# Attention on TensorE: both score products first, then both raw tiles

## The chip, the cores and the metric

The kernel runs on one NeuronCore of a Trainium2 chip. The metric is the device time of one execution in microseconds; lower is better. Times of single instructions come from one profiled execution, which takes a little longer than the median of the unprofiled runs.

## What is computed

Two transformer layers on x of shape (8, 512, 256), each with an attention and a feed-forward part that a modulation vector scales and shifts. The part that matters here is the attention, once in each layer, 16 heads of 16 features, over 8 batches of 512 tokens:

```
q, k, v = h @ wq.T, h @ wk.T, h @ wv.T          # first layer: then rms, rope on q and k
scores = einsum('bhtd,bhsd->bhts', q, k) * scale
attn = softmax(scores, axis=-1)
y = einsum('bhts,bhsd->bhtd', attn, v)
```

The softmax needs the maximum of each query's row of scores.

## The kernel before

`program` runs `attention` for the first layer, `mlp0`, `attention` for the second layer and `experts` in turn. Each `attention` call writes one long instruction list for every engine by a loop over steps p; every engine has its own `step(p)`, and semaphores tie them together.

A step works on a pair of heads. A pair's two heads lie in the two halves of the rows of KT and QS: head a = 0 in rows 0 to 48, head a = 1 in rows 64 to 112 (`BLK * a`). 32 steps make a batch (PAIRS), 8 steps a group of four heads, called G. For a group the scores are computed twice:

- **raw(n)**, line 1068: for query tile tt and head a of a pair, the unscaled scores with queries on the output's rows, 128x512, into SM[:, n % 2]. VectorE takes the negated row maximum of it (**maximum**, line 853). Once 16 maxima of a group are there, VectorE turns them (line 860) and eight DMAs of SyncE's queue write them as one more row of QS (line 348). Step p issues raw 2p + 28 and 2p + 29 (AHEAD is 28), so the maxima run 14 steps ahead of their use. Raw n waits until the maximum of n - 2 is done (line 1064): SM has two buffers.
- **scores(S, a)**, line 1084: the transposed scores of step S, with the extra row of maxima as a 49th row of the product, into ST[:, u % 2, a]. ScalarE turns both heads' scores into P in one exponential of 128x1024 (line 624). The call with a = 1 comes first and holds the waits: for the exponential two steps back (line 1081), and in the first step of a group for the DMAs of the maxima (line 1079).

Behind these four products a step of TensorE issues what its place in the batch asks for, here called its block: `job` (projections to q, k, v, transposes; placed by the tables AT0 and AT1), **values** (line 1101, four column tiles of P by V, in the steps 3, 5, 6 and 8 of a group), or the transposes of y (line 1143, in step 9, so step 1 of the next group). VectorE's step takes, in this order, the normalising work on AV (lines 888 and 894, in step 10, so step 2), the layer norm's statistics, the maximum of raw 2p + 28, in one step of a group the turning of the maxima, and the maximum of raw 2p + 29; in the first layer copies and reductions stand around them (lines 879, 919, 924).

Raws go from n = 0 to 511, so steps -14 to 241 have raws; scores go from step 0 to 255. Both are in steps 0 to 241.

```
if n >= 2:
    pe.wait_ge(max_s, n - 1)
r = slice(BLK * a, BLK * a + 3 * HD)
nc.tensor.matmul(SM[:, n % 2, :], QS[b % 2][r, 2 * g + pair, tt * 128:tt * 128 + 128],
                 KT[b % 2][r, 2 * g + pair, :], start=True, stop=True).then_inc(raw_mm, 1)
```

In a step n is even for the first raw, which has a = 0, and odd for the second, which has a = 1.

Of the kernel before, what the change touches and what calls it, by code (L numbers as in the profile page):

```python
# [109 lines left out]
AHEAD = 28  # L110
# [48 lines left out]
def attention(nc, layer, d, keep, ahead=None):  # L159
# [4 lines left out]
    def slots_of(name, n):  # L164

        return EARLY[n][name] if n < len(EARLY) and name in EARLY[n] else tuple(PAIRS * n + o for o in AT[name])
# [18 lines left out]
    def group_at(p, late):  # L185

        G, r = divmod(p - late, 8)
        return G if r == 0 and 0 <= G < B * NG else None

    with ExitStack() as ctx:  # L190
# [60 lines left out]
        def out(name, n):  # L251

            done_sem, out_sem, k = turn_of(name, n)
            return out_sem, k
# [711 lines left out]
        def tensor_steps(pe):  # L966
# [87 lines left out]
            def raw(n):  # L1054

                if not 0 <= n < 16 * B * NG:
                    return
                G, t = divmod(n, 16)
                b, g = divmod(G, NG)
                pair, a, tt = t // 8, t % 2, (t % 8) // 2  # L1060
                if g == 0 and t == 0:
                    pe.wait_ge(qk_ld[b % 2], 192 * (b // 2 + 1))
                if n >= 2:
                    pe.wait_ge(max_s, n - 1)
                elif n == 0 and L0:
                    pe.wait_ge(*out("H3", 0))
# [4 lines that stand above are left out]
            def scores(S, a):  # L1071

                G, u = divmod(S, 8)
                b, g = divmod(G, NG)
                if L0 and S == 0 and a == 1:
                    pe.wait_ge(*out("V1", 0))
                    pe.wait_ge(*out("QK3", 1))
                if u == 0 and a == 1:
                    pe.wait_ge(row_ld[G % 2], 128 * (G // 2 + 1))
                if S >= 2 and a == 1:  # L1080
                    pe.wait_ge(exp_s, S - 1)
                pair, o = 2 * g + u % 2, (u // 2) * 128
                r = slice(BLK * a, BLK * a + QROWS)
                ins = nc.tensor.matmul(ST[:, u % 2, a, :], KT[b % 2][r, pair, o:o + 128], QS[b % 2][r, pair, :],  # L1084
                                       start=True, stop=True)
                if a == 0:
                    ins.then_inc(st_mm, 1)

            def values(G, st):

                b, g = divmod(G, NG)
                pe.wait_ge(exp_s, 8 * G + 2 * st + 2)
                if st == 0:
                    if g == 0:
                        pe.wait_ge(*out("V1", b))
                    if G >= 1:
                        pe.wait_ge(y_out, G)
                    elif L0:
                        pe.wait_ge(mod_moved, 3)
                for j in range(HG):  # L1100
                    ins = nc.tensor.matmul(AV[32 * j:32 * j + 32, :], V[b % 3][:, st, g * HG + j, :], P[:, st, j, :],  # L1101
                                           start=st == 0, stop=st == TT - 1)
                ins.then_inc(av_mm, 1)

            def modulation(i):

                l, m0, m1, to = mod_part[i]
                pe.wait_ge(wm_ld[i], 16)
                if i == 2:
                    pe.wait_ge(*out("H1", 0))  # L1110
                for m in range(m0, m1):
                    for k in range(FT):
                        ins = nc.tensor.matmul(to[:, (m - m0) * B:(m - m0) * B + B], wm[:, l, k, m * 128:m * 128 + 128], cs[:, l, k, :],
                                               start=k == 0, stop=k == FT - 1)
                ins.then_inc(mod_mm, 1)
# [6 lines left out]
            def step(p):  # L1122
                if L0 and p in MOD_AT:
                    modulation(MOD_AT.index(p))
                raw(2 * p + AHEAD)
                if 0 <= p < PAIRS * B:
                    scores(p, 1)
                    scores(p, 0)
                raw(2 * p + AHEAD + 1)
                name, n = jobs.get(p, ("", 0))  # L1130
                if name:
                    job(name, n, (0, 1) if len(slots_of(name, n)) == 1 else (1,))
                elif p in begun:
                    job(*begun[p], (0,))
                for st, late in enumerate((3, 5, 6, 8)):
                    G = group_at(p, late)
                    if G is not None:
                        values(G, st)
                G = group_at(p, 9)
                if G is not None:  # L1140
                    pe.wait_ge(y_cp, G + 1)
                    for tt in range(TT):
                        ins = nc.tensor.transpose(AV[:, tt * 128:tt * 128 + 128], ysb[:, tt * 128:tt * 128 + 128], id32[:, :])
                    ins.then_inc(y_mm, 1)
                if group_at(p, 10) is not None and PAIRS * B - 58 <= p < PAIRS * B - 12 and p not in jobs and p not in begun:
                    free = jobs[max(q for q in jobs if q < p)]
                    pe.wait_ge(*out(*free))
                    src = wp_h[:, :, :].rearrange("p k n -> p (k n)") if L0 else keep["spare2"][:, 0:T]
                    for k in range(3):
                        nc.tensor.matmul(X[:, :], id16[:, :], src, start=True, stop=True)  # L1150
# [1289 lines left out]
```

## Time and profile before

| | |
|---|---|
| median of 3 runs | 1984.94 us (1984.57 to 1988.12) |
| the profiled execution | 1994.66 us |
| its span, first to last instruction | 1993.0 us |
| TensorE busy | 1820.3 us (91%) |
| VectorE busy | 1345.1 us (67%) |
| ScalarE busy | 1150.1 us (58%) |
| GpSimd busy | 654.5 us (33%) |
| mean granted TensorE clock | 0.954 |
| row maxima, line 853 | 1024, 654.4 us, 683 ns each |
| exponentials, line 624 | 512, 523.6 us, 1025 ns each |
| raws, line 1068 | 1024, 354.9 us busy |
| scores, line 1084 | 1024, 300.3 us busy |
| values, line 1101 | 2048 records, 275.2 us busy |

Shares are over the whole span, which has stages with different limits: the first attention call has scores from 108.0 us on, the second until 1681.9. Busy times of one line are times in which at least one of its instructions ran; TensorE overlaps its products, so the sum over lines says little of its pace. A product with values is recorded twice. Idle time is put down to what ended it.

### The profile page before, as it was taken

The page shows a single profiled execution, that of the slowest core. Times are in us where ns is not written, and L with a number is a line of the kernel's source. Part 1 is how long each engine was busy: PE and PEld are TensorE (multiplying, and loading weights), DVE is VectorE, ACT ScalarE, POOL GpSimd, SP SyncE. Part 2 cuts the span into 40 slices and gives each one's busy share as a digit, 9 for nine tenths or more (in the row PEclk, how much of TensorE's full clock was granted, in tenths as well). Part 3 has the DMA queues.
Part 4 walks back from the last instruction along what each step waited for, and adds up shares of the span by engine and source line. Part 5 has one row for each costly group of instructions (what it writes and reads, how often), then busy time and mean ns, then how long its engine had stood idle before and what let it go on. Part 6 is the DMA issues. An engine that isn't in the chain of part 4 may idle for free. (4 is left out here: it accounts for less than half of the span.)

```text
span 1993.0 us, 29496 instructions
## 1 busy us (share of the span) xinstructions
PE 1820.3 (91%) x10344; PEld 754.6 (38%) x10344; DVE 1345.1 (67%) x2598; ACT 1150.1 (58%) x1553; POOL 654.5 (33%) x918
## 2 busy tenths in 40 slices
PE   4789999999979999999999997899999997499998
PEld 3323333332224444444444443223233322355554
DVE  5488889888744535535535542688888884689993
ACT  4368778876743333424334232478778776477774
POOL 5667687761220000000000112234444311335452
PEclk8689999999989999999999998699999999699999
DMA  3345545444262000000001004333332320624410
GB/s 118 64 93 123 136 120 123 107 108 99 86 219 98 22 11 12 22 1 22 22 1 48 11 11 75 53 75 71 68 67 59 65 38 29 232 79 144 158 44 32
DMA packets 119620, 147.65 MB, mean 74 GB/s; under 512 B 19779, under 2 KB 102838, under 8 KB 117430
## 3 DMA queue, kind: packets, MB, share of 16 engines
q1 hardware_dynamic: 119478, 145.79, 27.7%
q8 instruction: 85, 1.39, 0.3%
q14 instruction: 57, 0.47, 0.1%
HBM read 100.34 MB, written 45.14 MB: 73 GB/s over the span
## 5 line engine op out<-in xcount | busy, mean ns | idle before, releaser
L853 DVE TENSOR_REDUCE A_M<-A_SM 128x1 f16<-128x512 f32 x1024 | 654.4, 683 | 137.8 <-PE A_SM L1068 135.2
L624 ACT ACTIVATE A_P<-A_ST 128x1024 f32<-128x1024 f32 x512 | 523.6, 1025 | 166.1 <-PE A_ST L1084 161.8
L1068 PE MATMUL A_SM<-A_KT,A_QS 48*128 48x512 f16 x1024 | 354.9, 399 | 45.2 <-DVE A_M L853 37.5
L1619 PE MATMUL B_PA<-B_Hh,B_wh 128*128 128x512 f16 x1024 | 388.1, 379 | 3.1 <-DVE B_Hl L1584 3.1
L1619 PE MATMUL B_PA<-B_Hl,B_wh 128*128 128x512 f16 x1024 | 388.1, 379 | 0.0
L1538 ACT ACTIVATE B_af<-B_PA,B_sv 128x512 f32<-128x512 f32 x192 | 131.9, 687 | 357.2 <-PE B_PA L1619 357.0
L1084 PE MATMUL A_ST<-A_QS,A_KT 49*128 49x512 f16 x1024 | 300.3, 386 | 2.6 <-DMA A_QS<-A_rows 2.1
L1101 PE MATMUL A_AV<-A_P,A_V 128*32 128x512 f32 x2048 | 275.2, 609 | 4.2 <-ACT A_P L624 3.6
L1582 DVE TENSOR_SCALAR B_Hh<-B_af 128x512 f16<-128x512 f32 x128 | 62.8, 490 | 278.8 <-ACT B_af L1538 278.8
L1068 PEld LDWEIGHTS A_SM<-A_KT,A_QS 48*128 48x128 f16 x1024 | 83.3, 93 | 432.7 <-DVE A_M L853 382.1
L1333 POOL TENSOR_TENSOR B_hl<-B_hf,B_hh 128x512 f16<-128x512 f32 x14 | 16.2, 1156 | 506.4 <-ACT B_hh L1349 506.4
L1619 PEld LDWEIGHTS B_PA<-B_Hh,B_wh 128*128 128x128 f16 x1024 | 100.2, 98 | 122.2 <-DVE B_Hl L1584 3.6
L1619 PEld LDWEIGHTS B_PA<-B_Hl,B_wh 128*128 128x128 f16 x1024 | 100.2, 98 | 118.8
L1584 DVE SCALAR_TENSOR_TENSOR B_Hl<-B_af,B_Hh 128x512 f16<-128x512 f32 x128 | 88.6, 692 | 4.4
L1101 PEld LDWEIGHTS A_AV<-A_P,A_V 128*32 128x32 f32 x2048 | 40.5, 108 | 79.5 <-issue 63.6
L972 PE MATMUL A_X<-A_wh,A_hh 128*128 128x256 f16 (+1 forms) x160 | 51.5, 322 | 12.6 <-ACT A_V L663 7.4
L1084 PEld LDWEIGHTS A_ST<-A_QS,A_KT 49*128 49x128 f16 x1024 | 55.4, 94 | 18.1 <-ACT A_P L624 9.4
L1538 ACT ACT_TABLE_LOAD x23 | 29.5, 1283 | 56.2 <-PE B_PA L1619 42.9
L1576 DVE SCALAR_TENSOR_TENSOR B_uf<-B_PD,B_sv,B_af 128x512 f32<-128x512 f32 x64 | 47.8, 746 | 18.9 <-ACT B_af L1538 13.7
L2249 PE MATMUL D_PA<-D_gh,D_eh 128*128 128x512 f16 x128 | 49.5, 386 | 4.9 <-POOL D_gl L1929 4.9
L516 POOL TENSOR_TENSOR A_ysq<-A_yn 128x256 f32<-128x256 f32 x32 | 19.6, 612 | 101.5 <-DVE A_yn L894 101.5
L2141 DVE SCALAR_TENSOR_TENSOR D_Hl<-D_af,D_Hh 128x512 f16<-128x512 f32 x64 | 43.0, 713 | 14.6 <-ACT D_Hh L2002 14.5
(362 smaller groups left out, 3246.1 us busy)
## 6 DMA issues: line engine op xcount, KB each, us to landing
D_w_st<-in_we_dram SPq DMA_DIRECT2D x16, 1024.0 KB, 7.2
qk<-A_tr SPq DMA_DIRECT2D x58, 256.0 KB, 2.5
A_KT<-qk SPq DMA_DIRECT2D x96, 128.0 KB, 5.0
A_QS<-qk SPq DMA_DIRECT2D x96, 128.0 KB, 4.9
A_w_st<-in_w_ffn_dram SPq DMA_DIRECT2D x32, 352.0 KB, 3.4
A_QS<-A_rows SPq DMA_DIRECT2D x512, 0.5 KB
w_hi<-A_f_hi SPq DMA_DIRECT2D x32, 176.0 KB, 3.4
w_lo<-A_f_lo SPq DMA_DIRECT2D x32, 176.0 KB, 3.9
```

Source lines behind the costliest of these rows:

```text
L624: nc.scalar.activation(P[:, st, 2 * pair:2 * pair + 2, :], ST[:, u % 2, :, :], ACT.Exp, scale=1.0 / math.sqrt(HD)).then_inc(exp_s, 1)
L853: nc.vector.tensor_reduce(M[G % 2][:, o:o + 1], SM[:, n % 2, :], AX, ALU.max, negate=True).then_inc(max_s, 1)
L972: ins = nc.tensor.matmul(out, a, c, start=first and n_ == 0, stop=last and n_ == len(todo) - 1)
L1068: nc.tensor.matmul(SM[:, n % 2, :], QS[b % 2][r, 2 * g + pair, tt * 128:tt * 128 + 128], KT[b % 2][r, 2 * g + pair, :], start=True, stop=T ...
L1084: ins = nc.tensor.matmul(ST[:, u % 2, a, :], KT[b % 2][r, pair, o:o + 128], QS[b % 2][r, pair, :], start=True, stop=True)
L1101: ins = nc.tensor.matmul(AV[32 * j:32 * j + 32, :], V[b % 3][:, st, g * HG + j, :], P[:, st, j, :], start=st == 0, stop=st == TT - 1)
L1538: nc.scalar.activation(af[:, s % 3, :], PA[:, s % 4, :], ACT.Silu if s < HM else ACT.Gelu, scale=sv[:, which, m:m + 1]).then_inc(a_out, 1)
L1576: nc.vector.scalar_tensor_tensor(out=uf[:, s % 2, :], in0=PD[:, s % 2, :], scalar=sv[:, 1, s:s + 1], in1=src, op0=ALU.mult, op1=ALU.mult). ...
L1582: nc.vector.tensor_scalar(Hh[w][:, m, :], src, HS, None, ALU.mult).then_inc(high, 1)
L1584: nc.vector.scalar_tensor_tensor(out=Hl[w][:, m, :], in0=src, scalar=HS, in1=Hh[w][:, m, :], op0=ALU.mult, op1=ALU.subtract).then_inc(spli ...
L1619: ins = nc.tensor.matmul(out, a, c, start=start and kt == 0 and n_ == 0, stop=stop and kt == kts[-1] and n_ == len(ops) - 1)
L2249: ins = nc.tensor.matmul(out, a, c, start=start and n_ == 0, stop=stop and n_ == len(ops) - 1)
```

## The change

In TensorE's `step`, the first raw moves behind the two scores. Nothing else is changed.

```diff
             def step(p):
                 if L0 and p in MOD_AT:
                     modulation(MOD_AT.index(p))
-                raw(2 * p + AHEAD)
                 if 0 <= p < PAIRS * B:
                     scores(p, 1)
                     scores(p, 0)
+                raw(2 * p + AHEAD)
                 raw(2 * p + AHEAD + 1)
                 name, n = jobs.get(p, ("", 0))
                 if name:
```

The order of the other engines and queues is the same. On TensorE, in the second call, at the first step of a group and the one behind it (A_SM is the raw tile, A_ST the scores, A_AV the values, A_X the bank of the jobs; A0_max counts VectorE's maxima, A0_row_ld the DMAs of the row of maxima, A0_exp the exponentials), before:

```order
L1068 MATMUL A_SM<-A_KT,A_QS 128x512 [waits A0_max]
L1084 MATMUL A_ST<-A_QS,A_KT 128x512 [waits A0_exp,A0_row_ld1]
L1084 MATMUL A_ST<-A_QS,A_KT 128x512
L1068 MATMUL A_SM<-A_KT,A_QS 128x512 [waits A0_max]
L1101 MATMUL A_AV<-A_P,A_V 32x512 [waits A0_exp]
L1101 MATMUL A_AV<-A_P,A_V 32x512 x3
L1068 MATMUL A_SM<-A_KT,A_QS 128x512 [waits A0_max]
L1084 MATMUL A_ST<-A_QS,A_KT 128x512 [waits A0_exp]
L1084 MATMUL A_ST<-A_QS,A_KT 128x512
L1068 MATMUL A_SM<-A_KT,A_QS 128x512 [waits A0_max]
```

and with the change:

```order
L1084 MATMUL A_ST<-A_QS,A_KT 128x512 [waits A0_exp,A0_row_ld1]
L1084 MATMUL A_ST<-A_QS,A_KT 128x512
L1068 MATMUL A_SM<-A_KT,A_QS 128x512 [waits A0_max] x2
L1101 MATMUL A_AV<-A_P,A_V 32x512 [waits A0_exp]
L1101 MATMUL A_AV<-A_P,A_V 32x512 x3
L1084 MATMUL A_ST<-A_QS,A_KT 128x512 [waits A0_exp]
L1084 MATMUL A_ST<-A_QS,A_KT 128x512
L1068 MATMUL A_SM<-A_KT,A_QS 128x512 [waits A0_max] x2
L1045 MATMUL A_X<-id,A_yn 128x128 [waits A0_y_out,A0_job_out]
```

The raw that stood ahead of the scores, and of their wait for the exponential and the row of maxima, now stands behind both; the two raws with their waits for the maxima are neighbours (x2), and the values follow the second raw as before.

Two steps on, where a projection with three products follows, before:

```order
L1068 MATMUL A_SM<-A_KT,A_QS 128x512 [waits A0_max]
L1084 MATMUL A_ST<-A_QS,A_KT 128x512 [waits A0_exp]
L1084 MATMUL A_ST<-A_QS,A_KT 128x512
L1068 MATMUL A_SM<-A_KT,A_QS 128x512 [waits A0_max]
L972 MATMUL A_X<-A_hh,A_wh 128x512 [waits A0_h_low,A0_job_out]
L972 MATMUL A_X<-A_hl,A_wh 128x512
L972 MATMUL A_X<-A_hh,A_wl 128x512
```

and with the change:

```order
L1084 MATMUL A_ST<-A_QS,A_KT 128x512 [waits A0_exp]
L1084 MATMUL A_ST<-A_QS,A_KT 128x512
L1068 MATMUL A_SM<-A_KT,A_QS 128x512 [waits A0_max] x2
L972 MATMUL A_X<-A_hh,A_wh 128x512 [waits A0_h_low,A0_job_out]
L972 MATMUL A_X<-A_hl,A_wh 128x512
L972 MATMUL A_X<-A_hh,A_wl 128x512
```

The first raw has changed places with the two scores; the block of projections keeps its place behind the second raw.

## Rows read from the trace of the kernel before

**Rows 1.** Stages: us from the start: length, busy us (instructions), clock, DMA share, GB/s
```profile
108.00:540.00 432.00, 404.70 (x2709) 128.97 (x2708) 376.46 (x696) 333.72 (x439) 264.96 (x317) 0.98 0.47 113
1269.50:1665.00 395.50, 375.22 (x2496) 114.83 (x2496) 333.36 (x622) 303.05 (x359) 131.02 (x266) 0.99 0.31 61
```

**Rows 2.** Who waited for whom, 1269.5 to 1665: us, times, longest
```profile
ACT A_P L624 <- PE A_ST L1084: 78.4, 131, 1.8
DVE A_M L853 <- PE A_SM L1068: 58.9, 124, 2.1
```

**Rows 3.** Who waited for whom, 108 to 540
```profile
DVE A_M L853 <- PE A_SM L1068: 39.5, 84, 2.2
```

**Rows 4.** Timeline, TensorE, second call: start us, us, instruction, [idle before]
```profile
1364.38 0.39 PE L1068 MATMUL A_SM<-A_KT,A_QS 48*128 48x512 f16 x1
1364.38 0.60 PE L1084 MATMUL A_ST<-A_QS,A_KT 49*128 49x512 f16 x2
1364.61 0.38 PE L1068 MATMUL A_SM<-A_KT,A_QS 48*128 48x512 f16 x1
...
1365.92 0.39 PE L1068 MATMUL A_SM<-A_KT,A_QS 48*128 48x512 f16 x1
1366.15 0.39 PE L1068 MATMUL A_SM<-A_KT,A_QS 48*128 48x512 f16 x1
...
1367.70 0.39 PE L1068 MATMUL A_SM<-A_KT,A_QS 48*128 48x512 f16 x1
1367.93 0.38 PE L1068 MATMUL A_SM<-A_KT,A_QS 48*128 48x512 f16 x1
...
1369.27 0.39 PE L1068 MATMUL A_SM<-A_KT,A_QS 48*128 48x512 f16 x1
1369.87 0.39 PE L1068 MATMUL A_SM<-A_KT,A_QS 48*128 48x512 f16 x1
...
1371.41 0.38 PE L1068 MATMUL A_SM<-A_KT,A_QS 48*128 48x512 f16 x1
...
1372.48 0.39 PE L1068 MATMUL A_SM<-A_KT,A_QS 48*128 48x512 f16 x1
1372.96 0.39 PE L1068 MATMUL A_SM<-A_KT,A_QS 48*128 48x512 f16 x1
1374.27 0.39 PE L1068 MATMUL A_SM<-A_KT,A_QS 48*128 48x512 f16 x1
...
1376.04 0.39 PE L1068 MATMUL A_SM<-A_KT,A_QS 48*128 48x512 f16 x1
1377.76 0.39 PE L1068 MATMUL A_SM<-A_KT,A_QS 48*128 48x512 f16 x1
```

**Rows 5.** Timeline, VectorE, the same group
```profile
1364.81 1.29 DVE L853 TENSOR_REDUCE A_M<-A_SM 128x1 f16<-128x512 f32 x2 [0.67 <-PE A_SM L1068]
...
1368.44 0.68 DVE L853 TENSOR_REDUCE A_M<-A_SM 128x1 f16<-128x512 f32 x1
```

**Rows 6.** Timeline of the first call, VectorE, and one row of TensorE
```profile
334.41 0.65 DVE L853 TENSOR_REDUCE A_M<-A_SM 128x1 f16<-128x512 f32 x1
...
336.60 0.68 DVE L919 TENSOR_REDUCE A_rv<-A_sq 128x32 f32<-128x512 f32 x1
...
338.88 0.69 DVE L853 TENSOR_REDUCE A_M<-A_SM 128x1 f16<-128x512 f32 x1 [0.41 <-PE A_SM L1068]
...
335.12 0.39 PE L1068 MATMUL A_SM<-A_KT,A_QS 48*128 48x512 f16 x1
```

**Rows 7.** The line of the scores, whole span: idle until, us, times
```profile
  DMA A_QS<-A_rows: 5.6, 9
```

**Rows 8.** Groups by line, 1269.5 to 1665: busy us, mean ns, idle before
```profile
L1101 PE MATMUL A_AV<-A_P,A_V 128*32 128x512 f32 x960 | 128.7, 608 | 0.0
```

**Rows 9.** Timeline, TensorE's weight loads, second call
```profile
1377.76 0.09 PEld L1068 LDWEIGHTS A_SM<-A_KT,A_QS 48*128 48x128 f16 x1 [0.42 <-DVE A_M L853]
1377.76 0.11 PEld L1084 LDWEIGHTS A_ST<-A_QS,A_KT 49*128 49x128 f16 x2
```

## The prediction

> **What bounds the kernel now.** I read the stage view first, then who waits for whom in each attention stretch, then the timeline of one group of eight steps. The change touches only the steps that issue both scores and raws: steps 0 to 241 of each of the two attention calls, 242 steps or 30.25 groups of eight per call. By the stage view [rows 1] these take 432.0 us in the first call and 395.5 us in the second, with TensorE busy 94% and 95% of that and VectorE 87% and 84%, at a granted clock of 0.98 and 0.99. A busy TensorE there is an engine that has something in it, not one at its peak, so the waits decide. In the second call VectorE's row maxima sat idle until TensorE's raw product 124 times, 58.9 us in all [rows 2]; in the first call 84 times, 39.5 us [rows 3]. So neither engine runs without a break: they hand two buffers (the two halves of SM) back and forth. I call the raw of the even number A and the other B.
>
> **The loop, in numbers.** All from one group of the second call, steps 0 to 7 from 1364.38 [rows 4]. (1) A and the first score start together (1364.38), the second score and B together 0.23 later (1364.61): they lie in different halves of the rows, so four products cost two slots of 0.23 us. (2) The maximum of A starts 0.43 after A (1364.81) [rows 5]. (3) Two maxima in a row take 1.29 us, one 0.69, so the second starts 0.60 after the first [rows 5]. (4) A raw that waits for its buffer starts 0.06 after the maximum that frees it: 334.41 + 0.65 = 335.06, the raw at 335.12 [rows 6]. A maximum's start to the raw that follows in its buffer is 0.68 + 0.06 = 0.74. (5) From B to the next step's first product is the step's own block: 1.31 with values, 1.55 with the transposes of step 1, 1.34 and 1.07 with three products in steps 2 and 4, 1.72 with six in step 7 [rows 4].
>
> If no product waits, B of the next step can't start before A + 0.43 + 0.60 + 0.74 = A + 1.77. That is the one limit that the change moves.
>
> **The change, part by part.** It adds and removes nothing; instruction counts, operands, DMAs and the orders of VectorE, ScalarE and the queues stay. Four products still make two pairs from different halves: both scores, then both raws. Cost of the pairs themselves: 0. What moves is A: it now starts 0.23 behind the step's first product, B where it was. Before, A and B were 0.23 apart and the scores filled that; VectorE got A first and was at work on it while B ran. Now both raws come together, and VectorE, which takes 0.60 per tile, gets its first tile 0.23 later.
>
> Worked for a step whose start P nothing delays. Before: A = P, so the next B is free at P + 1.77, and wants to start at P + 0.23 + block + 0.23; it waits if the block is under 1.31. After: A = P + 0.23, so B is free at P + 2.00 and wants the same place; it waits if the block is under 1.54. A block of values (1.31), half of all steps, just fits before and costs 0.23 after. In the step behind such a wait A and B are 0.23 apart again, the maxima start no later against B than before, and the next B waits for nothing new. So of a run of such steps about every second one pays 0.23.
>
> The whole group by this recurrence, starting with both buffers free (VectorE idle, as it is at 1364.38; step 2's first maximum is held by the normalising work ahead of it, to 0.74 after the step's start at 1367.70 [rows 4, 5]):
>
> | step | start before | waits of B | start after | waits of B |
> |---|---|---|---|---|
> | 0 | 0.00 | 0 | 0.00 | 0 |
> | 1 | 1.54 | 0 | 1.54 | 0.23 |
> | 2 | 3.32 | 0 | 3.55 | 0 |
> | 3 | 4.89 | 0.40 | 5.12 | 0.40 |
> | 4 | 6.83 | 0 | 7.06 | 0 |
> | 5 | 8.13 | 0.24 | 8.36 | 0.47 |
> | 6 | 9.91 | 0 | 10.37 | 0 |
> | 7 | 11.45 | 0 | 11.91 | 0.23 |
> | end | 13.40 | | 14.09 | |
>
> The trace has 1377.76 - 1364.38 = 13.38 for it, and the waits of B at steps 3 and 5 (0.60 and 0.48 from A to B in place of 0.23 [rows 4]), so the recurrence holds for before. It gives **+0.69 us per group**: three payments of 0.23. The same working with empty blocks in steps 2, 4 and 7, as at the end of the call, gives +0.69 too, since the payments sit in the same places.
>
> Second call: 30.25 x 0.69 = 20.9 us. First call: here VectorE has more to do between the maxima. Around 336.60 a further reduction of 0.68 us keeps it from idling until 338.88, where it waits 0.41 for a raw [rows 6]. While it is behind, it takes A late anyway and the 0.23 is hidden by its own backlog; the same recurrence over the group from 328.60 pays once, +0.23. I scale by the stalls: 84 against 124, 0.69 x 84 / 124 = 0.47 a group, 14.1 us. Bounds for the first call are 0.23 and 0.69 a group, 7 and 21 us.
>
> Side effects. The scores of a group's first step wait for the row of maxima that a DMA brings; that wait now holds A as well, which used to go ahead of it. It occurs 9 times, 5.6 us in all [rows 7]; what A could do meanwhile is at most 0.23 each, so 0 to 2 us, taken as 0 because the DMA chain itself starts with the same maxima. The exponential starts up to 0.23 earlier in its step. Nothing gains: the products with values, which need it, waited 0.0 us in all in the second call [rows 8].
>
> Sum: 20.9 + 14.1 = **+35 us**. On the profiled execution's own 1994.66 us (span 1993.0) that is 2029.7; this execution lies 9.7 above the median of the runs, 1984.94, so the median should be **2020 us**, 1.8% more.
>
> **A rule against the trace.** The second score's weights are in the same rows as those of A, which runs when they are loaded (1377.76, both score loads within 0.11 us), and the pairs still follow at 0.23 [rows 9, 4]. So a weight load behind a product in the same rows costs nothing here. The Trainium skill (TensorE: Matmul & The Clock Gate, section The mechanism) says that a weight load overlaps a running product only when the row group differs. By that rule the new order, in which the second score and A share a half and stand next to each other, would expose one load per step. The trace speaks against it for the old order, which has the same neighbours one product further apart.
>
> **Rivals.**
> - *The load shows.* If A's load can't start under the second score, each of the 484 steps takes the 0.09 us of one load more [rows 9]: 484 x 0.09 = 44 us on top, 2064. Chance 0.04.
> - *Hidden anyway.* Where VectorE never idles the delay costs nothing, as in five of the eight steps from 328.60. If my 0.06 and 0.43 are a little too long, the values block covers the delay: about 1985. Against it: 208 stalls that start exactly when a raw is done. Chance 0.06.
> - *Faster: ScalarE is what paces.* It sat idle before the exponential for 78.4 us, 131 times, in the second call until scores were done [rows 2]. If the chain scores, exponential, values ended last, each such wait would shrink by the 0.23 by which the second score moves ahead: 131 x 0.23 = 30 us, twice that for both calls, 1925. It decides from the point at which the values wait for the exponential; they waited 0.0 us [rows 8]. Chance 0.05.
> - *Every stall pays.* All (124 + 84) stalls grow by 0.23 and none is absorbed: 48 us, 2033; with the 2 us of the rows, 2035. Chance 0.05, the range's upper end.
>
> **How the numbers follow.** The forecast and the band around it have 0.80. Its low end is two payments a group in the second call (0.46 x 30.25 = 14 us) and none in the first: 1999, rounded down to 1998 for the runs' own scatter. The range 1998 to 2035 holds 0.85, the forecast and the last rival, and leaves out the three others. A measurement here can tell 0.2% (4 us) from no change: slower 0.89 (forecast, the load, every stall), same 0.06, faster 0.05.
>
> **What would show it.** Right: in the second call a group like the one from 1364.38 takes about 14.1 us in place of 13.4; VectorE's idle time behind raws grows by some 20 us there and about 14 in the first call, with more waits of TensorE before B; both raws start together after a long block, the first maximum 0.66 behind the step's start; the stretches without raws are unchanged. Wrong: an idle time of VectorE that stays near 59 and 40 us, pairs further apart than 0.23, values that wait for the exponential, or a longer time in the other stages.

## The result and the profile after

The change made the kernel slower: 2010.75 us (median of 4 runs, 2008.82 to 2012.26) against 1984.76 us (4 runs, 1983.48 to 1988.12), a ratio of 1.0116 with a 95% interval of 1.0095 to 1.0138. That is +26 us, where +35 was forecast. The profiled execution took 2011.95 us, with a span of 2010.2, 1.2 above its median; that of before lay 9.9 above its own. So the two traces differ by 17.3 us only, and they have to be compared stage by stage, and where the granted clock was the same.

The stages of the changed kernel (length, busy us of TensorE, weight loads, VectorE, ScalarE, GpSimd, then clock, DMA share, GB/s). First and third are steps 0 to 241 of the two attention calls; the second reaches from the end of the first call to the first raw of the second, the last from the last scores to the end:

```profile
109.70:546.80 437.10, 410.64 (x2709) 132.71 (x2708) 376.39 (x695) 331.86 (x439) 265.26 (x317) 0.99 0.46 112
565.20:1241.10 675.90, 650.03 (x3101) 306.30 (x3097) 310.71 (x636) 235.55 (x332) 45.85 (x53) 0.99 0.12 37
1268.90:1684.40 415.50, 391.63 (x2499) 119.24 (x2496) 333.95 (x623) 302.23 (x360) 131.01 (x266) 0.99 0.29 58
1701.20:2010.20 309.00, 264.75 (x1474) 148.96 (x1470) 233.60 (x442) 195.06 (x299) 133.66 (x169) 0.94 0.32 114
```

Of before the two attention stretches are [rows 1], and the two others:

```profile
558.60:1237.80 679.20, 650.28 (x3101) 306.34 (x3097) 314.47 (x636) 235.55 (x332) 45.60 (x53) 0.99 0.12 36
1681.90:1993.00 311.10, 267.85 (x1474) 150.24 (x1470) 233.56 (x442) 195.08 (x299) 134.01 (x169) 0.91 0.33 113
```

The second call's stretch grew from 395.5 to 415.5 us, the first call's from 432.0 to 437.1. TensorE's busy time grew along (375.2 to 391.6 in the second call), though its products are the same: it has something in it for longer. The untouched stages are 3.3 and 2.1 us shorter in this execution, the last at a granted clock of 0.94 in place of 0.91; that isn't the change's doing, and it is a part of what the traces lack against the medians.

The clock hides a part of the first call's loss as well. One group of eight steps of it (its 24th), before and with the change, in the columns of the rows above; the third number from the end is the granted clock:

```profile
442.72:458.75 16.03, 13.59 (x77) 3.05 (x77) 13.09 (x25) 8.70 (x10) 6.70 (x6) 0.79 0.67 215
447.48:461.02 13.54, 11.12 (x78) 3.10 (x78) 12.55 (x24) 7.93 (x10) 6.84 (x6) 1.00 0.66 206
```

The first ran 6.8 us of its time at the lower of the clock's two levels (1.2 GHz), the second none; a raw had waited 1.43 us for a maximum just before, at 448.54. This isn't tied to the order either: e1 below, as fast as the kernel before, took 13.03 us for this group at full clock.

The call's first group ran 10.9 us at the lower level before and 8.9 with the change (18.47 and 17.12 us in all). From step 0 to step 240, the first call ran 17.7 us at the lower level before and 8.9 with the change. So its growth over these 30 groups, 429.6 to 433.8 us, is too small a number for what the order costs.

The 28 groups that ran wholly at full clock in both traces are 8.0 us longer in sum, 0.28 a group. Against the kernel before, the same 28 groups are 8.0 us longer in e2 and 8.3 in e10, which have the new order in the first call, and 0.5 and 0.6 us shorter in e1 and e5, which lack it there (e5 has the old order in this call, e1 has A between the scores). In the second call 28 groups at full clock are 16.6 us longer, 0.59 a group. Taken for 30 groups each, that makes 8.5 and 17.7, an estimate of 26 us: what the medians differ by.

Who waited for whom in the second call's stretch, against [rows 2]:

```profile
DVE A_M L853 <- PE A_SM L1068: 80.5, 130, 2.8
ACT A_P L624 <- PE A_ST L1084: 80.3, 111, 1.8
```

and in the first call's, against [rows 3]:

```profile
DVE A_M L853 <- PE A_SM L1068: 51.3, 102, 1.2
```

VectorE's idle time behind raws rose by 21.6 us in the second call (58.9 to 80.5) and by 11.8 in the first (39.5 to 51.3). Now the group that the prediction worked through, TensorE from 1369.54 (of before: [rows 4]):

```profile
1369.54 0.39 PE L1084 MATMUL A_ST<-A_QS,A_KT 49*128 49x512 f16 x2
1369.77 0.38 PE L1068 MATMUL A_SM<-A_KT,A_QS 48*128 48x512 f16 x2
1370.08 1.06 PE L1101 MATMUL A_AV<-A_P,A_V 128*32 128x512 f32 x8
1371.08 0.39 PE L1084 MATMUL A_ST<-A_QS,A_KT 49*128 49x512 f16 x2
1371.31 0.61 PE L1068 MATMUL A_SM<-A_KT,A_QS 48*128 48x512 f16 x2
1371.85 0.66 PE L1045 MATMUL A_X<-id,A_yn 128*128 128x128 f32 x4
1372.34 0.60 PE L1143 MATMUL A_AV<-id,A_ysb 128*128 128x128 f32 x4
1372.88 0.39 PE L1084 MATMUL A_ST<-A_QS,A_KT 49*128 49x512 f16 x2
...
1374.43 0.39 PE L1084 MATMUL A_ST<-A_QS,A_KT 49*128 49x512 f16 x2
...
1376.36 0.39 PE L1084 MATMUL A_ST<-A_QS,A_KT 49*128 49x512 f16 x2
...
1377.65 0.39 PE L1084 MATMUL A_ST<-A_QS,A_KT 49*128 49x512 f16 x2
1377.88 0.86 PE L1068 MATMUL A_SM<-A_KT,A_QS 48*128 48x512 f16 x2
1379.67 0.39 PE L1084 MATMUL A_ST<-A_QS,A_KT 49*128 49x512 f16 x2
1379.89 0.38 PE L1068 MATMUL A_SM<-A_KT,A_QS 48*128 48x512 f16 x2
...
1381.20 0.39 PE L1084 MATMUL A_ST<-A_QS,A_KT 49*128 49x512 f16 x2
1381.43 0.61 PE L1068 MATMUL A_SM<-A_KT,A_QS 48*128 48x512 f16 x2
...
1383.38 0.39 PE L1084 MATMUL A_ST<-A_QS,A_KT 49*128 49x512 f16 x2
```

Both raws are one row (x2) at 1369.77, 0.23 behind the scores, and VectorE's first maximum starts at 1370.19, 0.65 after the step's start, where it was 0.43 [rows 5]:

```profile
1370.19 1.29 DVE L853 TENSOR_REDUCE A_M<-A_SM 128x1 f16<-128x512 f32 x2 [0.89 <-PE A_SM L1068]
1371.72 1.29 DVE L853 TENSOR_REDUCE A_M<-A_SM 128x1 f16<-128x512 f32 x2 [0.25 <-PE A_SM L1068]
```

A row with x2 and 0.38 us is a pair that started together; with 0.61 (1371.31, 1381.43) B came 0.23 after A, because it waited for its buffer; with 0.86 (1377.88), 0.48 after. The starts of the steps, from the group's own start:

| step | 0 | 1 | 2 | 3 | 4 | 5 | 6 | 7 | end |
|---|---|---|---|---|---|---|---|---|---|
| forecast | 0 | 1.54 | 3.55 | 5.12 | 7.06 | 8.36 | 10.37 | 11.91 | 14.09 |
| measured | 0 | 1.54 | 3.34 | 4.89 | 6.82 | 8.11 | 10.13 | 11.66 | 13.84 |
| before | 0 | 1.54 | 3.32 | 4.89 | 6.80 | 8.10 | 9.89 | 11.43 | 13.38 |

From step 2 on, forecast and measured differ by 0.21 to 0.25: of the three payments of 0.23 the ones of steps 5 and 7 came as forecast, that of step 1 was made (0.61 at 1371.31) and swallowed in the same step. What swallowed it shows in the weight loads of that step's second transposes, before and with the change, and in ScalarE's rows with the change:

```profile
1367.11 0.42 PEld L1143 LDWEIGHTS A_AV<-id,A_ysb 128*128 128x128 f32 x4 [0.22 <-ACT A_ysb L686]
1372.27 0.43 PEld L1143 LDWEIGHTS A_AV<-id,A_ysb 128*128 128x128 f32 x4
```

```profile
1371.13 0.60 ACT L714 ACTIVATE A_xn<-rare,A_shift,A_rstd 128x256 f32<-128x256 f32 x1
1371.62 0.59 ACT L686 ACTIVATE A_ysb<-A_AV 128x512 f32<-128x512 f32 x1
```

The second transposes need ScalarE's copy of AV, which stands behind a normalisation of the layer norm in ScalarE's queue. Before, they waited 0.22 us for it. With the change the copy ends at 1371.62 + 0.59 = 2.67 after the group's start, as before (1366.46 + 0.59), and TensorE, 0.22 later by then, no longer waits. The block of 1.55 us, which I had taken for work, had this wait in it.

This group is also the cheapest of the second call's kinds. Four kinds follow each other there. From B of step 0 to B of the next step 0 they take, in turn, 12.77, 13.08, 13.17 and 13.38 us before, and 13.42, 13.70, 13.78 and 13.84 with the change: 0.65, 0.62, 0.61 and 0.46 more. (From step start to step start it reads otherwise, 12.39, 13.08, 13.54 and 13.38 before and 12.22, 13.70, 14.98 and 13.84 after, because a step now starts with its scores, ahead of a raw that waits.)

### The profile page after: what moved, and what is told of

Same layout as the page of the kernel before. It is cut to its first block and busy times, and to the rows that moved or that the text cites. A ratio compares the mean times of both kernels' runs of the same rounds, so it can differ in the third digit from the quotient of the medians.

```text
span 2010.2 us, 29496 instructions
## 1 busy us (share of the span) xinstructions
PE 1837.0 (91%) x10344; PEld 761.2 (38%) x10344; DVE 1340.8 (67%) x2598; ACT 1145.8 (57%) x1553; POOL 654.2 (33%) x918
## 5 line engine op out<-in xcount | busy, mean ns | idle before, releaser
L853 DVE TENSOR_REDUCE A_M<-A_SM 128x1 f16<-128x512 f32 x1024 | 656.0, 684 | 169.7 <-PE A_SM L1068 166.7
L624 ACT ACTIVATE A_P<-A_ST 128x1024 f32<-128x1024 f32 x512 | 517.8, 1024 | 158.3 <-PE A_ST L1084 156.5
L1068 PE MATMUL A_SM<-A_KT,A_QS 48*128 48x512 f16 x1024 | 299.1, 393 | 56.7 <-DVE A_M L853 49.1
L1084 PE MATMUL A_ST<-A_QS,A_KT 49*128 49x512 f16 x1024 | 204.0, 388 | 1.6 <-DMA A_QS<-A_rows 1.1
L1084 PEld LDWEIGHTS A_ST<-A_QS,A_KT 49*128 49x128 f16 x1024 | 50.0, 93 | 273.9 <-ACT A_P L624 152.7
L686 ACT ACTIVATE A_ysb<-A_AV 128x512 f32<-128x512 f32 x64 | 38.2, 597 | 33.0 <-PE A_AV L1101 33.0
```

What stands on the lines that cost most here:

```text
L624: nc.scalar.activation(P[:, st, 2 * pair:2 * pair + 2, :], ST[:, u % 2, :, :], ACT.Exp, scale=1.0 / math.sqrt(HD)).then_inc(exp_s, 1)
L853: nc.vector.tensor_reduce(M[G % 2][:, o:o + 1], SM[:, n % 2, :], AX, ALU.max, negate=True).then_inc(max_s, 1)
```

## The experiments

All ratios are against the kernel before, run on the same chip beside them.

**e1: A between the scores.** TensorE issues the first score, A, the second score, B.

```diff
-                raw(2 * p + AHEAD)
                 if 0 <= p < PAIRS * B:
                     scores(p, 1)
+                raw(2 * p + AHEAD)
+                if 0 <= p < PAIRS * B:
                     scores(p, 0)
                 raw(2 * p + AHEAD + 1)
```

> First score (a = 1), then raw A, then the second score, then raw B. My theory: what counts is that A starts with the step and that something fills the 0.23 us to B. Here both hold, so the time is that of before within 0.2% (1985), VectorE's idle time behind raws near 59 us in the second call and 40 in the first. Rival 'the load shows' or any price of products of the same half standing next to each other (here the order of halves is 1, 0, 0, 1, as in the change): up to the change's whole +26 us, 2011.

Measured: 0.9993 (0.9977 to 1.0010), no difference. Its TensorE at a group's start in the second call:

```profile
1360.39 0.39 PE L1084 MATMUL A_ST<-A_QS,A_KT 49*128 49x512 f16 x1
1360.39 0.60 PE L1068 MATMUL A_SM<-A_KT,A_QS 48*128 48x512 f16 x2
1360.62 0.38 PE L1084 MATMUL A_ST<-A_QS,A_KT 49*128 49x512 f16 x1
```

First score and A start together at 1360.39, second score and B at 1360.62 (the row of raws, x2, spans both). VectorE's idle time behind raws over the whole program is 133.7 us, against 135.2 before and 166.7 with the change. So a raw behind the first score's wait costs nothing, nor does the order of halves 1, 0, 0, 1.

**e2: the change, with the scores swapped.** The order of halves is 0, 1, 0, 1.

```diff
                 if 0 <= p < PAIRS * B:
-                    scores(p, 1)
                     scores(p, 0)
+                    scores(p, 1)
                 raw(2 * p + AHEAD)
                 raw(2 * p + AHEAD + 1)
```

(`scores` takes its waits at a = 0 and its signal at a = 1 there.)

> As the change, but the score of head a = 0 comes first, and takes the waits along, and the one of a = 1 behind it, which tells ScalarE; so the halves alternate 0, 1, 0, 1 as before. Theory: nothing depends on the neighbours' halves, so the time is that of the change, 2011 within 0.3%, and both raws start 0.23 us behind the step's first product. Rival 'the load shows': the cost goes away, 1985 to 1990.

Measured: 1.0116 (1.0087 to 1.0145), the same as the change. The two pairs are 0.23 apart as with the change:

```profile
1365.63 0.39 PE L1084 MATMUL A_ST<-A_QS,A_KT 49*128 49x512 f16 x2
1365.86 0.38 PE L1068 MATMUL A_SM<-A_KT,A_QS 48*128 48x512 f16 x2
```

With e1 this settles the first rival: a weight load behind a product of the same half shows in no order tried here, so the sentence of the Trainium skill (TensorE: Matmul & The Clock Gate, section The mechanism) that such loads overlap only across row groups did not decide anything in this kernel.

**e3 and e4: maxima over half the keys**, in the old order and in the new one. The row maximum is one of the first 256 keys' scores; all else is computed.

```diff
-                nc.vector.tensor_reduce(M[G % 2][:, o:o + 1], SM[:, n % 2, :], AX, ALU.max, negate=True).then_inc(max_s, 1)
+                nc.vector.tensor_reduce(M[G % 2][:, o:o + 1], SM[:, n % 2, 0:T // 2], AX, ALU.max, negate=True).then_inc(max_s, 1)
```

> The old order, but each row maximum reads only the first 256 of the 512 keys (the maximum is then one over half the keys; everything else is computed). VectorE's time per tile falls from 0.60 to about 0.33 us, and a buffer is free again 0.27 us earlier. Theory: the waits of TensorE before B go away almost wholly: 393 to 361 us in the second call and 430 to 395 in the first, so about 1920 in all. It is the base for the next run. Rival (TensorE paces the calls by itself): less than 10 us gained.

> The order of the change with the same half maxima. Theory: the limit on B is now A + 0.43 + 0.33 + 0.47 = A + 1.23, so blocks of 1.31 cover it in both orders and the change costs little: 0 to +8 us against the run before it, where it costs 26 with whole maxima. Rival (the cost lies in TensorE's own order, in pairs, weight loads or waits in its queue): +26 us here as well.

Measured: e3 0.9798 (0.9772 to 0.9823), e4 0.9796 (0.9769 to 0.9822). With a faster VectorE the timing can't tell the two orders apart: of the change's 26 us at most some 10 can be left by the two intervals, as expected (0 to 8), and the rival that puts all of it into TensorE's own order falls. By the traces the second call is 6.3 us longer in the new order (362.5 to 368.8 us from the start of step 0 to that of step 240; with whole maxima 393.3 to 412.2), the first 3.7 us shorter (419.9 to 416.2). Here too the clock was not the same: in the groups at full clock in both, the new order is 4.7 us longer over 29 groups of the second call and 2.9 us over 22 of the first.

The size of e3 was missed: some 1946 us where 1920 was expected. The second call did what was expected (393.3 to 362.5 us), the first call gained only 9.7 us (429.6 to 419.9) of 35. Two things stand there. The first call ran at a mean granted clock of 0.96 in place of 0.98 (34.7 us at the lower level, 17.7 before); in 23 groups at full clock in both it gained 14.9 us, 0.65 a group. And steps that shorten run into the DMAs that bring the row of maxima. The scores' line waited for them in e3, and in e4:

```profile
  DMA A_QS<-A_rows: 17.9, 17
```

```profile
  DMA A_QS<-A_rows: 36.2, 36
```

against 5.6 us in 9 waits before [rows 7]; of the 17.9 us of e3, 14.4 lie in the first call. So with half maxima a second limit begins to show, some 40 us below the time of before, and in the first call it may hide a remainder of the order's cost. In the second call this remainder is about a quarter of what it was at full clock (0.16 us a group against 0.59).

**e5: the new order in the second call alone**, `if L0` keeping the old one.

> The new order in the second call alone (first call as before). The trace of the change has the second call's groups 0.63 us longer each, the first call's 0.14. Theory: the two calls are independent, so this run has about +19 to +20 us, 2005; the groups of the second call take 12.23, 13.70, 14.98 and 13.84 us in turn as with the change. Rival (the second call's extra time comes from something the first call leaves behind): less.

Measured: 1.0109 (1.0081 to 1.0136), +22 us. Its second call's groups take 12.22, 13.69, 14.98, 13.84 us in turn, as with the change. Over 28 of them at full clock it is 16.3 us longer than before, the change 16.6.

**e10: the new order in the first call alone.**

> The new order in the first call alone. By the trace of the change the first call is some 5 us longer, and the run with the new order in the second call alone had +1.09%. Theory (the parts add up): +0.1 to +0.4%, 1987 to 1993. Rival (an interaction of the calls): outside that.

Measured: 1.0054 (1.0033 to 1.0076), +11 us, above what was expected from the trace of the change. That expectation rested on the 5 us by which the first call's whole stretch had grown, and those hid a difference in clock. In this run's own trace the stretch from step 0 to step 240 took 435.1 us, +5.5; in the 28 groups at full clock in both it is 8.3 us longer, as with the change (8.0). The two single ratios add up to 1.63%, the change has 1.16%; the three intervals just allow that the parts add up. The traces add up: 16.3 and 8.3 us for the parts, 16.6 and 8.0 for the whole, each over 28 groups.

**e6: both raws first.**

```diff
                 raw(2 * p + AHEAD)
+                raw(2 * p + AHEAD + 1)
                 if 0 <= p < PAIRS * B:
                     scores(p, 1)
                     scores(p, 0)
-                raw(2 * p + AHEAD + 1)
```

> Raw A, raw B, then both scores. A now starts with the step, as before, but B starts with it too, with nothing between them. Theory (the limit on B, 1.77 us behind the A of the step before, has to be covered by what TensorE does between that A and this B; here the scores' slot lies behind B, so a block under 1.54 leaves 0.23 us open again): slower than before by as much as the change or more, +20 to +45 us, since the recurrence has +23 in the second call and +19 in the first, and the exponentials come later in place of earlier. Rival (what costs is that A, and so VectorE's first maximum, comes late behind the scores): no change, 1985, or faster.

Measured: 1.0213 (1.0174 to 1.0252), +42 us. A is as early as it can be, and the kernel is slower than with the change:

```profile
1384.22 0.39 PE L1068 MATMUL A_SM<-A_KT,A_QS 48*128 48x512 f16 x2
1384.45 0.38 PE L1084 MATMUL A_ST<-A_QS,A_KT 49*128 49x512 f16 x2
...
1385.76 0.62 PE L1068 MATMUL A_SM<-A_KT,A_QS 48*128 48x512 f16 x2
```

At 1385.76 the pair of raws lasts 0.62: B waited 0.23 for its buffer, and here the scores queue behind it. So it isn't A's lateness in itself. What counts is that TensorE has something to do between A and B. Its groups at full clock are 20.7 us longer than before in the second call (29 of them) and 12.7 in the first (28), where the recurrence had +23 and +19.

**e7: the new order in step 4 of each group alone.**

> The new order only in step 4 of every group, one step in eight, in both calls. Step 4's block is short in the second call (1.07 or 1.18 us) and step 5's B waits there already. Theory: each group of the second call pays the full 0.23, +6.7 us, and the first call, where step 4 mostly has a block of 1.72, +2.4: together +9, 1994. Rival (the cost is spread evenly over all steps): 26 / 8 = +3 us.

Measured: 1.0056 (1.0036 to 1.0077), +11 us. The rival had 3 us, below the interval (7 to 15 us), so the cost isn't spread evenly: one step in eight makes a third to a half of the cost of all eight. In the groups at full clock in both traces the second call is 6.3 us longer over 29, where 6.7 was expected, and the first 2.0 over 27, where 2.4 was. The group that takes 13.38 us before takes 13.61 here:

```profile
1362.47 0.39 PE L1084 MATMUL A_ST<-A_QS,A_KT 49*128 49x512 f16 x2
1362.69 0.38 PE L1068 MATMUL A_SM<-A_KT,A_QS 48*128 48x512 f16 x2
...
1363.86 0.39 PE L1068 MATMUL A_SM<-A_KT,A_QS 48*128 48x512 f16 x1
...
1364.46 0.39 PE L1068 MATMUL A_SM<-A_KT,A_QS 48*128 48x512 f16 x1
...
1369.27 0.39 PE L1068 MATMUL A_SM<-A_KT,A_QS 48*128 48x512 f16 x1
```

(1355.66 to 1369.27.) Step 4's pair starts at 1362.69, and B of step 5 waits from 1363.86 to 1364.46, 0.60 in place of 0.48. In the first call step 4 mostly has a block of 1.71 to 1.74 us, over the 1.54 that the recurrence asks for, and most of these groups keep their time within 0.03 us (13.39 and 13.38, 14.68 and 14.69). Six groups at full clock have a block of 0.87 to 0.95 there, and each pays 0.21 or 0.22 (12.82 to 13.04). In the second call the block is 1.18 us or less in 29 of the 30 groups, and each of the 29 pays 0.16 to 0.23. That is the threshold of the prediction seen from both sides.

**e8: the new order where the recurrence has it for nothing** (steps 0 and 2 of the first call's groups, 2 and 3 of the second's).

> The new order only in steps 0 and 2 of the first call's groups and 2 and 3 of the second call's, where the recurrence of TensorE and VectorE has it for nothing (+0.2 and 0 us). What is left is the exponential, which starts 0.21 us earlier there. If the earlier ScalarE gives something back where a block waits for it (as the first call's groups suggest, 14.68 before and 14.44 with the change), this is faster than before by up to 6 us; if not, 1985 within 0.2%.

Measured: 1.0010 (0.9996 to 1.0025), no difference. These steps are free, as the recurrence has it, but nothing that the timing can tell is to be had there; at full clock its groups are 1.0 us shorter in the first call, which is within what e1 and e5 scatter, and equal in the second. No order tried beats the kernel before.

**e9: the change, with ScalarE started as late as before.**

```diff
                 act.wait_ge(st_mm, S + 1)
+                if 2 * S + AHEAD < 16 * B * NG:
+                    act.wait_ge(raw_mm, 2 * S + AHEAD + 1)
```

> The order of the change, but the exponential of a step also waits until that step's raw A is done, 0.21 to 0.23 us after the scores, so ScalarE starts where it did before the change. My recurrence of TensorE and VectorE alone has +15 us in the first call and +18 to +21 in the second; the change measured about +5 and +20 by its trace. Theory (in the first call, and in step 1 of many groups of the second, the earlier exponential gives back what the late raw costs): slower than the change by 5 to 12 us, 2016 to 2023, with the groups of the first call 0.2 us or more longer, and step 1 of the second call's group from 1364.38 on 0.2 us longer. Rival (the first call's small loss comes from VectorE's backlog alone, or from waits for the DMAs of the maxima that shrink): as the change, 2011.

Measured: 1.0163 (1.0126 to 1.0200), 2018.73 us against the change's 1.0116. 5 to 12 us was expected, and some 9 is what the ratios differ by, but this can't be counted for the order. The intervals touch, and the runs had different clocks: e9's six ran at mean granted clocks of 0.953 to 0.962, the change's four at 0.961 to 0.963, and at 0.962 the two took 2012.27 and 2011.95 us.

The traces tell it apart better. From step 0 to step 240 the first call took 429.6 us before, 433.8 with the change and 438.5 here; the second 393.3, 412.2 and 411.1. Of the 4.7 us between the last two in the first call, 3.2 lie in two groups of which e9 ran more at the lower clock (17.54 us against 15.32, and 18.12 against 17.12). Over the 28 groups at full clock in both, e9 is 1.6 us longer. What of this comes back the same way each time is the third group of a batch: in four batches it went from 14.68 us or a little more to 14.44 or 14.47 with the change and back to 14.71 or 14.74, 1.1 us in all. TensorE's waits in the first call for what ScalarE takes out of X with its line 637 (639 in e9, whose lines are numbered two higher) are of that size. Before and in e9 (us, times, longest; with the change there is no such row for the products):

```profile
PE A_X L972 <- ACT A_hf L637: 1.6, 4, 0.4
PE A_X L974 <- ACT A_hf L639: 1.0, 4, 0.3
```

One place of it is step 2 of the group from 313.92, where the projection with wp waits for ScalarE to have emptied X. Before, with the change, and in e9, the second raw or the pair and the projection:

```profile
317.86 0.38 PE L1068 MATMUL A_SM<-A_KT,A_QS 48*128 48x512 f16 x1
318.63 0.39 PE L972 MATMUL A_X<-A_yTh,A_wp_h 128*128 128x512 f16 x1 [0.39 <-ACT A_hf L637]
```

```profile
319.97 0.59 PE L1068 MATMUL A_SM<-A_KT,A_QS 48*128 48x512 f16 x2
320.55 0.39 PE L972 MATMUL A_X<-A_yTh,A_wp_h 128*128 128x512 f16 x1
```

```profile
321.22 0.50 PE L1070 MATMUL A_SM<-A_KT,A_QS 48*128 48x512 f16 x2
321.99 0.39 PE L974 MATMUL A_X<-A_yTh,A_wp_h 128*128 128x512 f16 x1 [0.26 <-ACT A_hf L639]
```

The wait of 0.39 us is gone with the change and 0.26 is back in e9. So the earlier exponential does give something back, but 1 to 2 us, not 5 to 12, and with it held back the first call is still only some 8 us longer than before over 27 groups at full clock, not the 15 us of the recurrence for the whole call. The other half of the expectation missed too: step 1 of the second call's group is no longer in e9 than with the change (the group takes 13.84 both times). The change had not moved the exponential ahead of that copy: it starts 0.69 us after the group's start before (1365.07) and with the change (1370.23), behind another copy of ScalarE's.

## Why the prediction was right, and where it was off

- **The limit A + 1.77.** Right. In the group from 1369.54 B waits as the recurrence has it, 0.23 more in steps 1, 5 and 7; e7 shows one such payment alone, e6 the same limit with A early (A at 1384.22, the next B 0.23 behind 1385.76, so at A + 1.77), e3 and e4 that most of the cost goes with VectorE's time per tile.
- **The pairs cost nothing.** Right: 0.23 us between the pairs in every order.
- **Second call, 0.69 a group.** 18.9 us over 30 groups, 0.63 a group (393.3 to 412.2); at full clock 0.59. The groups without jobs at the call's end pay 0.67 (12.70 to 13.37). The one group that the recurrence was worked on paid 0.46: "1.55 with the transposes of step 1" was entered as a block of work, and 0.22 of it is a wait for ScalarE, which takes in B's 0.23. The other kinds, 0.61 to 0.65 a group, came nearer to the 0.69, and they had not been worked out; that the sum fits so well is in part luck.
- **First call, 0.47 a group, "bounds 7 and 21 us".** This is the term that was mis-sized: 0.28 a group at full clock, some 8.5 us in place of 14.1, within its bounds. "I scale by the stalls" assumed that a stall costs the same in both calls. But by the recurrence itself the order costs nothing where a step's block is 1.54 or more, and in the first call 68 of 240 blocks are that long before, in the second 24. e7 shows it for step 4, free at blocks of 1.72 and 0.21 or 0.22 at short ones; for the other steps it is argued, not shown. Where the recurrence was worked out it held: for the group from 328.60 it had +0.23, and from B of step 0 to the next B of step 0 that group went from 14.44 to 14.67. VectorE's idle time grew by 11.8 us, near the 14 forecast, though only some 8.5 us of them became time.
- **"Nothing gains."** Not quite. The products with values waited 0.0 us, but their weight loads, which the prediction did not read, had waited for the exponential 13 times in the second call, 5.6 us, and 4 times, 1.1 us, with the change. No run prices that; a load's wait can lie beside a product that still runs. And ScalarE works through a queue: behind an exponential that starts 0.21 us earlier, its copies out of X start earlier too, and projections wait for these. e9 prices all that an earlier exponential gives at 1 to 2 us in the first call and nothing in the second.
- **The DMAs of the maxima, 0 to 2 us, taken as 0.** Nothing was lost there: the scores' waits for them went from 5.6 us in 9 [rows 7] to

```profile
  DMA A_QS<-A_rows: 2.8, 3
```

but they vary by as much between kernels of one speed (9.1 us in 13 waits in e1), so I count no gain from them.
- **The rivals.** The load that shows: refuted by e1 and e2. Hidden anyway: refuted by the result. ScalarE as what paces: refuted as a whole; a small part of it was real, 1 to 2 us by e9. Every stall pays: no; it would have been 48 us, 19 of them from the first call's 84 stalls, which cost 8.5.
- **Range.** 2010.75 lies well inside 1998 to 2035, below its middle, mostly by the first call's term.

## What to carry to other kernels

With two buffers between a producer and a consumer, order the producer's queue so that independent work fills the gap between the two fills; two fills side by side hand the consumer both tiles at once, and the limit of the next fill moves by the length of what was taken out of the gap. Whether that costs is read step by step: only where the work up to the next fill is shorter than the limit (here 1.54 us). When a block's duration is read from a timeline, look for waits inside it first, because these are what absorbs a delay; and follow an earlier start through the whole queue of the engine that it reaches, not to its first user alone. And before two traces are subtracted, look at the granted clock of the stretches: here 8.8 us more at the lower level in one of them hid half of the first call's loss, and groups at full clock in both gave it back.

## What was not expected of the hardware

Products that read different halves of the rows start together in every combination tried (score with raw, score with score, raw with raw), and pairs follow at 0.23 us whether the neighbours' halves alternate or repeat. A faster VectorE (0.42 us a tile in place of 0.68) brought 2.0% only. The scores then wait for the DMAs that write the row of maxima, 17.9 us in 17 waits in the old order and 36.2 us in 36 in the new one, and the first call's granted clock was 0.96 in place of 0.98; no run here separates the two.
